# First stage of a two-layer model: projections in the order keys, queries, values; heads loaded for four rows at once; squares summed on TensorE

## The chip, the cores and the metric

The kernel runs on one core of one Trainium2 chip. The metric is the time on the device in microseconds (us) for one execution; the time before is the median of three runs.

## The reference

The reference is a model of two layers; the change lies in layer 0, in the part ahead of a recurrence.

```python
x = _layernorm(hidden_states)                       # 8 rows of 512 tokens, 128 channels
q = l2norm(silu(short_conv(x @ Wq.T, cq)).reshape(b, l, 16, 8))
k = l2norm(silu(short_conv(x @ Wk.T, ck)).reshape(b, l, 16, 8))
v = silu(short_conv(x @ Wv.T, cv)).reshape(b, l, 16, 8)
lr = softplus(x @ Wlr.T + 1e-3)
# 32 chunks of 16 tokens, each step needs the state of the one before:
#   two softmaxes over the state, an output, two rounds of an attention-like update
o = lax.scan(step, (W_in0, W_out0), chunks(q, k, v, lr))
attn = layernorm_per_head(o) * (x @ Wg.T) @ Wo.T
# mixture of experts on the same x: top 2 of 8 experts for each of 4096 tokens
logits = x @ W_router.T ; gates = top2(softmax(logits))
y = sum over experts of gate * (silu(x @ Wg_e) * (x @ Wu_e)) @ Wd_e
```

Layer 1 (a state-space scan and a second mixture of experts with a capacity) follows, and its code is not touched beyond two counts of a semaphore.

## The kernel before

The kernel is written engine by engine: SP issues the hardware DMAs, GpSimd (POOL) the scatters, and each engine's program is an order written out by hand, with semaphores between them. Nothing is planned by a program: what stands first in an engine's block runs first.

**Stage A, layer norm.** SP loads `x` in four pieces of 512 KB (L530 to L532), then seven small weights, then the three expert weights of 2 MB each (L538). VectorE waits for all four pieces (L1633), takes statistics of 32 tiles (L1545, L1548) and writes 32 normalised tiles (L1554). TensorE transposes them in groups of four (L860), ScalarE copies them to `xnT` (L1176). POOL meanwhile issues 28 DMAs of 260 KB that clear the slot tables (L711, L714).

**Stage B, projections and convolutions.** There are 24 units, numbered `cu`: for each of the eight rows b the query, the key and the value projection in turn (L865 to L870). A unit is a 128x512 product on TensorE into one of four banks, a first tap on ScalarE (L1188) into one of four buffers `cv`, three more taps on VectorE (L1642), SiLU on ScalarE (L1180), and a store of 256 KB to the DRAM scratch `qkv_scr` (L557). The first tap of unit cu waits until the store of unit cu-4 has landed, since both use one buffer (L1187). Once per row TensorE also makes the gate (L874) and the learning rates (L875), and SP loads the heads of the row before back from DRAM, in the layout of the recurrence, where partition (b, h) holds 8x512 values: K, V and Q of 256 KB each into the 16 partitions of that row (L545), and the learning rates (L548). SP's queue is one list: loads and stores are issued in this order.

**Stage C, routing.** After the last unit TensorE computes the router's logits for 32 tiles (L845, called at L877). VectorE then runs `dispatch(0)` (L1563 to L1620): softmax with one exponential on ScalarE (L1201), top 2, a mask, ranks by two matmuls (L851, L852, awaited at L1590), and the slots (`slots_ready`, L1620). POOL waits for the slots and issues 64 indirect DMAs (L727) that scatter the normalised rows to their slots. SP loads the first tiles of slots once all 64 have landed (L569, L574).

**Stage D, unit length.** ScalarE squares K (L1208) into `TMP`, VectorE sums over the 8 elements (L1654), and the same for Q with the one buffer; then root (L1211), reciprocal (L1658) and product (L1659). The learning rates pass through Abs, Exp and Ln on ScalarE (L1214 to L1216), and VectorE finishes them (L1661). SP waits for both sums before it loads expert tiles (L570), because `TMP` and the tiles share memory.

**Stage E, the recurrence.** 32 steps, mostly on VectorE (`step`, L1696 to L1823). Steps 4 to 27 are routed: TensorE, ScalarE and POOL run three expert tiles beside each step. The last step without tiles, step 3, already transposes the first tile: on TensorE `xg_T(4, 0)` and `up(4, 0)` stand ahead of `o_sums(3)` (L944 to L953), and on ScalarE the copy `xT(c + 1, 0)` stands ahead of the exponential `exp_q` (L1279 to L1281), for which VectorE waits at L1756. Two reciprocals stand in each half of a step: Z3 and ZK (L1725, L1727), Z2 and ZQ (L1796, L1759). In a routed step ScalarE writes the last result tile of the step before (`y(c - 1, 2)`, L1269) ahead of a table load and three SiLUs (L1271 to L1273), and then loads the table for the exponential `exp_2` (L1274, L1278), for which VectorE waits at L1792.

ScalarE enters step 0 after SP's 4 MB fill of `y_tok1` (L568) has landed (L1297), and TensorE enters it after the three expert weights (L881).

Of the kernel before, what the change touches and what calls it, by code (L numbers as in the profile page):

```python
# [107 lines left out]
def build(nc, d):  # L108
# [5 lines left out]
    with ExitStack() as ctx:  # L114
# [10 lines left out]
        qkv_scr = dram("qkv_scr", [3, P, T])  # L125
        lr_scr = dram("lr_scr", [2 * H, T])
# [76 lines left out]
        TMP = xnT[:].rearrange("p (e t) -> p e t", e=HD)  # L203
# [51 lines left out]
        MK, MQ, ZK, ZQ = (sb(n, [P, CH]) for n in ("MK", "MQ", "ZK", "ZQ"))  # L255
        M2, M3, Z2, Z3 = (sb(n, [P, 2 * DI]) for n in ("M2", "M3", "Z2", "Z3"))
# [51 lines left out]

        x_loaded = sem("x_loaded")
# [9 lines left out]
        xn_ready = sem("xn_ready")  # L319
        xnT_ps = sem("xnT_ps")  # L320
# [12 lines left out]
        heads_loaded = sem("heads_loaded")  # L333
# [107 lines left out]
        NCU = 3 * B  # L441
        ZEROED = 16 * (TILES_A // 4 + E * CAP // (4 * P))
# [86 lines left out]
        def _(sp):  # L529
            for g in range(4):  # L530
                sp.dma_start(x[:, 8 * g:8 * g + 8, :],
                             d["x"].rearrange("(i p) c -> p i c", p=P)[:, 8 * g:8 * g + 8, :]).then_inc(x_loaded, 16)  # L532
# [4 lines left out]
            for dst, src in ((wg_a, "wg_a"), (wu_a, "wu_a"), (wd_a, "wd_a")):  # L537
                sp.dma_start(dst[:], d[src]).then_inc(we_loaded, 16)  # L538

            def heads_load(b):  # L540

                for w, dst in ((1, K), (2, V), (0, Q)):
                    cu = 3 * b + w
                    sp.wait_ge(stored[cu % 4], 16 * (cu // 4 + 1))
                    sp.dma_start(dst[b * H:(b + 1) * H, :, :],  # L545
                                 qkv_scr[w].rearrange("(h e) (b t) -> b h e t", h=H, b=B)[b]).then_inc(heads_loaded, 16)
                sp.wait_ge(lr_stored[b % 2], 16 * (b // 2 + 1))
                sp.dma_start(LZ[b * H:(b + 1) * H, :, :],  # L548
                             lr_scr.rearrange("(h j) (b t) -> b h j t", h=H, b=B)[b]).then_inc(heads_loaded, 16)

            sp.wait_ge(xn_ready, NT)
            for cu in range(NCU):
                b, w = divmod(cu, 3)
                sp.wait_ge(silu_done, cu + 1)
                sp.dma_start(qkv_scr[w, :, b * L:(b + 1) * L], cv[:, cu % 4, :]).then_inc(stored[cu % 4], 16)  # L557
                if w == 0 and b >= 1:
                    sp.wait_ge(lr_copied, b)
                    sp.dma_start(lr_scr[:, (b - 1) * L:b * L], LR[0:2 * H, (b - 1) % 2, :]).then_inc(lr_stored[(b - 1) % 2], 16)  # L560
                if w == 2 and b >= 1:
                    heads_load(b - 1)
            sp.wait_ge(lr_copied, B)
            sp.dma_start(lr_scr[:, (B - 1) * L:B * L], LR[0:2 * H, (B - 1) % 2, :]).then_inc(lr_stored[(B - 1) % 2], 16)
            heads_load(B - 1)
# [4 lines left out]
            sp.wait_ge(norm2, 2)  # L570
# [117 lines left out]
        def _(pool):  # L688
# [29 lines left out]
            pool.wait_ge(xn_ready, NT)  # L718
# [52 lines left out]
            pool.wait_ge(xn_ready, 2 * NT)  # L771
# [68 lines left out]
        def _(pe):  # L840
# [13 lines left out]
            for g in range(G4):  # L854
                if g >= 2:
                    pe.wait_ge(xnT_copied, g - 1)
                for j in range(4):
                    i = 4 * g + j
                    pe.wait_ge(xn_ready, i + 1)
                    t = pe.transpose(ps[:, g % 2, j * P:(j + 1) * P], xn[:, i, :], ident[:])  # L860
                t.then_inc(xnT_ps, 1)
            pe.wait_ge(w_loaded, 16 * 7)
            for b in range(B):
                rhs = xnT[:, b * L:(b + 1) * L]
                pe.wait_ge(xnT_copied, b + 1)  # L865
# [12 lines left out]
            ranks(0)

# [106 lines left out]
            def turn(g):  # L986

                pe.wait_ge(xn_ready, NT + 4 * g + 4)
# [178 lines left out]
        def _(act):  # L1167
# [6 lines left out]
            for g in range(G4):  # L1174
# [8 lines left out]
            for cu in range(NCU):  # L1183
# [5 lines left out]
                if cu >= 1:  # L1189
                    silu(cu - 1)  # L1190
# [878 lines left out]
```

## Time and profile before

| | us |
|---|---|
| median of three runs | 1404.48 |
| lowest and highest | 1402.98, 1407.38 |
| the profiled execution, its own time | 1406.85 |
| its span in the trace | 1404.7 |
| VectorE busy in the span | 1254.6 (89%) |
| TensorE busy | 986.4 (70%) |
| ScalarE busy | 693.6 (49%) |
| GpSimd busy | 686.5 (49%) |

The share of busy time is a mean over stages. The 2.15 us between the span and the execution's own time lie around the span and are taken as unchanged. Times in the views count from the start of the span. A view of one engine in order of time gives for each row its start, its length, the operation, and in brackets how long the engine sat idle before it and what ended that.

### The profile page before, as it was taken

The page shows a single profiled execution, that of the slowest core. Times are in us where ns is not written, and L with a number is a line of the kernel's source. Part 1 is how long each engine was busy: PE and PEld are TensorE (multiplying, and loading weights), DVE is VectorE, ACT ScalarE, POOL GpSimd, SP SyncE. Part 2 cuts the span into 40 slices and gives each one's busy share as a digit, 9 for nine tenths or more (in the row PEclk, how much of TensorE's full clock was granted, in tenths as well). Part 3 has the DMA queues.
Part 4 walks back from the last instruction along what each step waited for, and adds up shares of the span by engine and source line. Part 5 has one row for each costly group of instructions (what it writes and reads, how often), then busy time and mean ns, then how long its engine had stood idle before and what let it go on. Part 6 is the DMA issues. An engine that isn't in the chain of part 4 may idle for free. (4 is left out here: it accounts for less than half of the span.)

```text
span 1404.7 us, 15886 instructions
## 1 busy us (share of the span) xinstructions
PE 986.4 (70%) x3590; PEld 577.2 (41%) x3591; DVE 1254.6 (89%) x2399; ACT 693.6 (49%) x1297; POOL 686.5 (49%) x623
## 2 busy tenths in 40 slices
PE   4671134778877777777762587668988898888874
PEld 2131032455555555555552562223434443444331
DVE  6767999999999999999989988999897888879899
ACT  2541312455455554455532327636576667666742
POOL 5001874222322223222211005788798789788895
PEclk9875556798899899999975668988999899999998
DMA  9998111000000000000052304446354435444346
GB/s 366 250 180 184 40 44 41 14 22 23 19 22 19 17 23 19 20 19 18 14 152 91 90 1 142 139 142 183 131 179 148 163 130 170 137 163 159 105 176 189
DMA packets 110082, 145.48 MB, mean 104 GB/s; under 512 B 26843, under 2 KB 82920, under 8 KB 105552
## 3 DMA queue, kind: packets, MB, share of 16 engines
q1 hardware_dynamic: 94448, 118.70, 29.3%
q0 software_dynamic: 9920, 21.12, 4.1%
q10 hardware_dynamic: 5664, 5.11, 1.2%
q8 instruction: 16, 0.26, 0.1%
q14 instruction: 34, 0.28, 0.1%
HBM read 108.06 MB, written 39.04 MB: 105 GB/s over the span
## 5 line engine op out<-in xcount | busy, mean ns | idle before, releaser
L1961 DVE TENSOR_TENSOR ps<-ps,cv 128x512 f32<-128x512 f32 x256 | 163.1, 682 | 24.8 <-ACT ps L1499 23.5
L1072 PE MATMUL ps<-Q,ident 128*128 128x512 f32 x256 | 140.5, 641 | 34.3 <-DVE Q L1979 21.2
L750 POOL DMA_INDIRECT y_tok<-xnT,meta x72 | 76.8, 1067 | 147.1 <-ACT xnT L1238 140.0
L727 POOL DMA_INDIRECT slots_x<-xn,sl_put x64 | 76.0, 1188 | 133.5 <-DVE sl_put L1620 114.3
L806 POOL TENSOR_TENSOR Q<-LR,xn 128x512 f32<-128x512 f32 x96 | 122.7, 1278 | 28.7 <-DVE LR L1970 13.1
L911 PE MATMUL ps<-wd_a,xn 128*128 x576 | 97.7, 321 | 36.7 <-ACT xn L1232 36.7
L921 PE MATMUL ps<-x,ident 128*128 128x64 f32 x512 | 74.0, 298 | 61.9 <-DVE x L518 52.2
L523 POOL TENSOR_TENSOR x<-x 128x512 f32<-128x512 f32 x27 | 31.8, 1176 | 174.5 <-DVE x L1763 174.5
L921 PEld LDWEIGHTS ps<-x,ident 128*128 128x128 f32 x512 | 73.3, 218 | 76.3 <-DVE x L518 56.8
L911 PEld LDWEIGHTS ps<-wd_a,xn 128*128 128x128 f32 x576 | 82.4, 220 | 50.5 <-issue 49.0
L894 PE MATMUL ps<-wg_a,xnT 128*128 x144 | 93.9, 739 | 12.3 <-issue 10.9
L1250 ACT ACTIVATE x<-x 128x128 f32<-128x128 f32 (+1 forms) x127 | 32.0, 277 | 133.4 <-DVE x L1822 60.9
L1970 DVE TENSOR_TENSOR_SCAN LR<-V,ps 128x512 f32<-128x512 f32 x64 | 77.6, 1212 | 14.3 <-ACT V L1458 12.4
L901 PE MATMUL ps<-ident,xn 128*128 128x128 f32 x288 | 47.6, 291 | 56.7 <-DVE xn L1708 56.7
L929 PE MATMUL ps<-x,ident 128*128 128x128 f32 x256 | 43.2, 323 | 62.6 <-DVE x L523 31.6
L1077 PE MATMUL ps<-Q,ident 128*128 128x512 f32 x144 | 80.2, 644 | 7.1 <-POOL Q L817 4.2
L1970 DVE TENSOR_TENSOR_SCAN LR<-wd_a,ps 128x512 f32<-128x512 f32 x64 | 77.5, 1211 | 5.0 <-POOL Q L806 2.8
L1072 PEld LDWEIGHTS ps<-Q,ident 128*128 128x128 f32 x256 | 47.9, 202 | 80.4 <-DVE Q L1979 29.5
L895 PE MATMUL ps<-wu_a,xnT 128*128 x144 | 80.3, 642 | 0.0
L1970 DVE TENSOR_TENSOR_SCAN Q<-wd_a,ps 128x512 f32<-128x512 f32 x64 | 76.6, 1197 | 0.9 <-POOL seg L817 0.5
L1970 DVE TENSOR_TENSOR_SCAN Q<-V,ps 128x512 f32<-128x512 f32 x64 | 76.5, 1196 | 0.0
L1224 ACT ACTIVATE xnT<-ps 128x128 f32<-128x128 f32 x72 | 19.5, 272 | 113.9 <-PE ps L887 113.9
(340 smaller groups left out, 2773.2 us busy)
## 6 DMA issues: line engine op xcount, KB each, us to landing
cv<-bc_scr SPq DMA_DIRECT2D x64, 512.0 KB, 3.9
xn<-bc_scr SPq DMA_DIRECT2D x24, 1024.0 KB, 4.7
O<-bc_scr SPq DMA_DIRECT2D x8, 1024.0 KB, 5.0
slots_x<-O POOLq DMA_DIRECT2D x28, 260.0 KB, 11.2
qkv_scr<-cv SPq DMA_DIRECT2D x24, 256.0 KB, 6.4
xnT<-slots_x SPq DMA_DIRECT2D x72, 64.0 KB, 1.8
x<-in_x SPq DMA_DIRECT2D x8, 512.0 KB, 5.8
y_tok<-O SPq DMA_DIRECT2D x1, 4096.0 KB, 17.6
```

What stands on the lines that cost most here:

```text
L727: pool.indirect_dma_start(out=slots_x, out_offset=bass.IndirectOffsetOnAxis(ap=sl_put[:, j, i:i + 1], axis=0), in_=xn_rows[:, i, :], in_of ...
L750: pool.indirect_dma_start(out=y_tok, out_offset=bass.IndirectOffsetOnAxis(ap=meta_bits[:, n, 0:1], axis=0), in_=yg[:, k, :], in_offset=Non ...
L806: pool.tensor_tensor(yc_g0[:, n % 4, :], st_g0[:, n % 2, :], cn, ALU.mult).then_inc(yc_ready, 1)
L894: pe.matmul(ps[:, 1 + 2 * k, :], xgT[:, k, :], wg_a[:, bass.ds(off, F)], start=True, stop=True).then_inc(gu_ps, 1)
L895: pe.matmul(ps[:, 2 + 2 * k, :], xgT[:, k, :], wu_a[:, bass.ds(off, F)], start=True, stop=True).then_inc(gu_ps, 1)
L901: t = pe.transpose(ps[:, 1 + 2 * k, f * P:(f + 1) * P], hid[:, k, f * P:(f + 1) * P], ident[:])
L911: m = pe.matmul(ps[:, 0, 0:D], hidT[:, k, f * P:(f + 1) * P], wd_a[:, bass.ds(off + f * D, D)], start=(f == 0), stop=(f == FC - 1))
L921: m = pe.matmul(ps[:, 7, 0:DI * CH], ident[:], PQ[:, e, :, :], start=(e == 0), stop=(e == HD - 1))
L1072: pe.matmul(ps[:, 4, :], ident[:], yc_g0[:, n % 4, :], start=(n == 0), stop=(n == NS - 1)).then_inc(y0_used, 1)
L1077: pe.matmul(ps[:, 5, :], ident[:], yo_g1[(units_before(c) + u) % 3], start=(u == 0), stop=(u == units(c) - 1)).then_inc(y1_used, 1)
L1961: tt(dBu(g), ps[:, 2 + g, :], b_rows[:, n % 4, :], ALU.mult).then_inc((inject0, b_used)[g], 1)
L1970: dve.tensor_tensor_scan(st(n, g), dA(k), dBu(g), 0.0, ALU.mult, ALU.add).then_inc(scanned, 1)
```

## The change

- The 24 units come in the order of eight key, eight query, eight value units (`CONVS`). A transposition stands between the first units, the learning rates go with the queries, four tiles of logits with each value unit. The gate products come after the routing's ranks, into the banks of the units.
- `qkv_scr` is laid out `[3, B, P, L]`, so that a store is one contiguous block, and the heads are loaded in six DMAs of 1 MB, each for four rows b, into 64 partitions. A load is issued after units 5, 9, 13, 17, 21 and at the end. The learning rates come back in one DMA.
- The expert weights are loaded after the heads, two of the three after a sum of squares. The slot tables are cleared after `x` has landed. VectorE starts statistics on each quarter of `x`.
- VectorE normalises 16 tiles and ScalarE the other 16.
- Squares go to `wd_a` and `wu_a`; the sum over 8 elements is eight matmuls with the identity. The reciprocal for K stands inside `dispatch`, after the mask.
- SP waits for `gate_copied` where it waited for the sums.
- In a step, Z3 and ZK share one reciprocal, and so do Z2 and ZQ. ScalarE loads the SiLU table and runs the first SiLU ahead of `y(c - 1, 2)`.

The core of the diff:

```diff
+        CONVS = [(w, b) for w in (1, 0, 2) for b in range(B)]
+            def heads_load(half, w):
+                for cu in range(4):
+                    sp.wait_ge(stored[cu], 16 * (2 * (1, 0, 2).index(w) + half + 1))
+                dst, done = ((Q, q_in), (K, k_in), (V, v_in))[w]
+                sp.dma_start(dst[half * 64:(half + 1) * 64, :, :],
+                             qkv_scr[w, 4 * half:4 * half + 4].rearrange("b (h e) t -> (b h) e t", h=H)).then_inc(done, 16)
+            for cu, (w, b) in enumerate(CONVS):
+                sp.wait_ge(silu_done, cu + 1)
+                sp.dma_start(qkv_scr[w, b], cv[:, cu % 4, :]).then_inc(stored[cu % 4], 16)
...
+                if cu % 4 == 1 and cu > 4:
+                    n = cu // 4 - 1
+                    heads_load(n % 2, CONVS[4 * n][0])
...
+            heads_load(1, 2)
+            sp.dma_start(wg_a[:], d["wg_a"]).then_inc(we_loaded, 16)
+            for n, (dst, src) in enumerate(((wd_a, "wd_a"), (wu_a, "wu_a"))):
+                sp.wait_ge(norm2, n + 1)
                 sp.dma_start(dst[:], d[src]).then_inc(we_loaded, 16)
...
-            sp.wait_ge(norm2, 2)
+            sp.wait_ge(gate_copied, B)
...
+            for g in range(4):
+                pool.wait_ge(x_in[g], 16)
...
+            def norms(n, sq, bank):
+                pe.wait_ge(squared, 4 * n + 4)
+                for e in range(HD):
+                    m = pe.matmul(ps[:, bank, :], ident[:], sq[:, e, :], start=(e == 0), stop=(e == HD - 1))
+                m.then_inc(norm2, 1)
+            turn0(0)
+            turn0(1)
             pe.wait_ge(w_loaded, 16 * 7)
             for b in range(B):
+                project(b)
+                if b + 2 < G4:
+                    turn0(b + 2)
+            for b in range(B):
+                project(B + b)
+                since(pe, lr_copied, b)
+                pe.matmul(ps[0:2 * H, 7, :], wlr[:], xnT[:, b * L:(b + 1) * L], start=True, stop=True).then_inc(lr_ps, 1)
+            for b in range(B):
+                project(2 * B + b)
+                m = logits(0, range(4 * b, 4 * b + 4), wrt[:])
+            m.then_inc(logits_ps, 1)
+            norms(0, sq_k, 6)
             ranks(0)
+            norms(1, sq_q, 7)
+            for b in range(B):
+                pe.wait_ge(conv_done, NCU)
+                since(pe, gate_copied, b - 3)
+                pe.matmul(ps[:, 2 + b % 4, :], wproj[:, 3 * P:4 * P], xnT[:, b * L:(b + 1) * L], start=True, stop=True).then_inc(gate_ps, 1)
...
+            for cu in range(2, NCU):
+                if cu + 1 < G4:
+                    xnT_copy(cu + 1)
+                silu(cu - 2)
+                tap(cu)
+                if B <= cu < 2 * B:
+                    lr_copy(cu - B)
+                k = cu - 2 * B - 2
+                if 0 <= k < 4:
+                    if k == 0:
+                        act.wait_ge(k_in, 32)
+                    square(K, sq_k, 2 * k)
...
+            norm_roots(0, 6)
+            act.wait_ge(q_in, 32)
+            for k in range(4):
+                square(Q, sq_q, 2 * k)
+            for b in range(B):
+                if b == 4:
+                    norm_roots(1, 7)
+                act.wait_ge(gate_ps, b + 1)
+                act.activation(gateT[:, b * L:(b + 1) * L], ps[:, 2 + b % 4, :], ACT.Copy).then_inc(gate_copied, 1)
...
+                if here:
+                    act.preload_act_table(ACT.Silu)
+                    silu_gate(c, 0)
                 if before:
                     y(c - 1, 2)
                 if here:
-                    act.preload_act_table(ACT.Silu)
-                    for k in range(TPS):
-                        silu_gate(c, k)
+                    silu_gate(c, 1)
+                    silu_gate(c, 2)
...
+                    if i % 8 == 0:
+                        dve.wait_ge(x_in[i // 8], 16)
...
                 tt(mask, oh[:, 0], oh[:, 1], ALU.add).then_inc(mask_ready, 1)
+                if layer == 0:
+                    unit_length_root(0)
...
-                o.wait(z_3)
-                r_3 = o.mark(dve.reciprocal(Z3[:, j:], Z3[:, j:]))
                 o.wait(z_k)
-                r_k = o.mark(dve.reciprocal(ZK[:], ZK[:]))
+                r_k = o.mark(dve.reciprocal(Z3K[:, j:], Z3K[:, j:]))
```

## Rows read from the trace of the kernel before

**Rows 1.** VectorE's waits, whole span: us in total, times, longest.

```profile
DVE cv L1642 <- ACT cv L1188: 19.0, 7, 3.4
DVE Z L1793 <- ACT x L1250: 5.8, 13, 0.5
```

**Rows 2.** VectorE in order of time, stages A to D.

```profile
10.58 6.28 DVE L1545 BATCH_NORM_STATS2 stats<-x 128x6 f32<-128x128 f32 x32 [10.58 <-DMA x<-in_x]
...
20.01 8.30 DVE L1554 TENSOR_SCALAR xn<-x,mv,rstd 128x128 f32<-128x128 f32 x32
...
30.39 9.08 DVE L1642 SCALAR_TENSOR_TENSOR cv<-ps,taps,cv 128x511 f32<-128x511 f32 x12 [2.00 <-ACT cv L1188]
...
97.53 4.54 DVE L1642 SCALAR_TENSOR_TENSOR cv<-ps,taps,cv 128x511 f32<-128x511 f32 x6 [2.42 <-ACT cv L1188]
110.09 0.42 DVE L1563 COPY O<-ps 128x256 f32<-128x256 f32 x1 [8.02 <-PE ps L845]
...
124.56 0.42 DVE L1591 COPY O<-ps 128x256 f32<-128x256 f32 x1 [2.16 <-PE ps L852]
...
132.29 0.20 DVE L1620 CAST sl_put<-slot 128x64 int32<-128x64 f32 x1
132.40 7.02 DVE L1654 TENSOR_REDUCE nrm<-xnT 128x512 f32<-128x4096 f32 x1
...
150.66 3.35 DVE L1658 RECIPROCAL nrm<-nrm 128x512 f32<-128x512 f32 x1
154.05 4.42 DVE L1659 TENSOR_TENSOR K<-K,nrm 128x4096 f32<-128x4096 f32 x1
...
167.42 0.18 DVE L1685 COPY WI<-X 128x32 f32<-128x32 f32 x1
```

**Rows 3.** ScalarE in order of time, stages B and C.

```profile
68.51 0.69 ACT L1188 ACTIVATE cv<-ps,taps 128x512 f32<-128x512 f32 x1 [4.31 <-DMA qkv_scr<-cv]
...
102.76 1.28 ACT L1201 ACT_TABLE_LOAD   x1
```

**Rows 4.** DMA: GB/s in 40 slices of 60 to 80 us, then of 0 to 20 us.

```profile
GB/s 102 119 98 111 119 94 115 119 90 119 107 189 254 369 402 381 324 205 98 111 119 94 115 115 98 111 115 102 115 184 193 229 340 361 369 315 234 119 127 119
...
GB/s 0 0 0 20 126 306 346 332 307 285 287 297 291 286 268 184 342 411 327 383 412 414 406 413 419 412 391 397 408 413 391 396 402 392 376 377 378 365 427 525
```

**Rows 5.** POOL in order of time: the first scatter and a long one.

```profile
133.31 1.02 POOL L727 DMA_INDIRECT slots_x<-xn,sl_put  x1 [114.30 <-DVE sl_put L1620]
...
155.01 4.31 POOL L727 DMA_INDIRECT slots_x<-xn,sl_put  x1 [0.31 <-issue]
```

**Rows 6.** All engines in order of time, step 3 of the recurrence.

```profile
232.33 0.33 SPq L574 DMA_DIRECT2D xnT<-slots_x  x1
...
234.52 0.47 PE L887 MATMUL ps<-ident,xnT 128*128 128x128 f32 x1 [6.09 <-DMA meta<-slots_x]
...
235.21 0.25 ACT L1250 ACTIVATE x<-x 128x64 f32<-128x64 f32 x1
...
235.60 0.21 DVE L1757 TENSOR_REDUCE ZQ<-x 128x16 f32<-128x64 f32 x1
```

**Rows 7.** The stores, line L557: from issue to landing.

```profile
DMA to landing us min/median/max: 2.0/6.4/8.6
```

**Rows 8.** TensorE in order of time: two projections (each is two passes).

```profile
38.69 1.98 PE L870 MATMUL ps<-xnT,wproj 128*128 128x512 f32 x4
```

**Rows 9.** Stretch 80:110: us; busy of PE, PEld, DVE, ACT, POOL; PEclk; DMA share; GB/s.

```profile
80.00:110.00 30.00, 25.40 (x80) 16.37 (x80) 16.13 (x22) 12.63 (x21) 0.00 (x0) 0.64 1.06 178
```

**Rows 10.** DMA issues: the fill of 4 MB, median us from issue to landing.

```profile
y_tok<-O SPq DMA_DIRECT2D x1, 4096.0 KB, 17.6
```

**Rows 11.** VectorE in order of time, the second half of a routed step.

```profile
410.26 0.19 DVE L1796 RECIPROCAL Z<-Z 128x8 f32<-128x8 f32 x1
410.38 0.21 DVE L1757 TENSOR_REDUCE ZQ<-x 128x16 f32<-128x64 f32 x1
410.62 0.25 DVE L1759 RECIPROCAL ZQ<-ZQ 128x16 f32<-128x16 f32 x1
```

More of the change, by code:

```diff
@@ L305, in s1_of @@
             return s1_later[:, c * L:(c + 1) * L] if c else wproj[:]
+        x_in = [sem(f"x_in{g}") for g in range(4)]
         x_loaded = sem("x_loaded")
@@ L553, in _ @@
[L553 to L562, printed above, removed]
@@ L1173, in _, with norm_rows, xnT_copy, tap @@
             act.activation(rstd[:], rstd[:], ACT.Sqrt).then_inc(ln_std, 1)
-            for g in range(G4):
+            act.wait_ge(ln_bias, 1)
+            def norm_rows(g):
+                for i in range(4 * g, 4 * g + 4):
+                    act.activation(xn[:, i, :], x[:, i, :], ACT.Identity, scale=rstd[:, i:i + 1], bias=nrm[:, 0, i:i + 1]).then_inc(xn_act, 1)
+            def xnT_copy(g):
                 act.wait_ge(xnT_ps, g + 1)
                 act.activation(xnT[:, g * 512:(g + 1) * 512], ps[:, g % 2, :], ACT.Copy).then_inc(xnT_copied, 1)
+            def tap(cu):
+                act.wait_ge(proj_ps, cu + 1)
+                if cu >= 4:
+                    act.wait_ge(stored[cu % 4], 16 * (cu // 4))
+                act.activation(cv[:, cu % 4, :], ps[:, 2 + cu % 4, :], ACT.Copy, scale=taps[:, CONVS[cu][0], 3:4]).then_inc(tap_first, 1)
             def silu(cu):
@@ L1649, in _, with unit_length @@
             dispatch(0)
-            dve.wait_ge(heads_loaded, 16 * 4 * B)
-            for n in range(2):
-                dve.wait_ge(squared, n + 1)
-                dve.tensor_reduce(nrm[:, n, :], TMP.rearrange("p e t -> p t e"), AX_X, ALU.add).then_inc(norm2, 1)
+            def unit_length(n, t):
+                o.mark(tt(t[:], t[:], bc(nrm[:, n, :], 1, HD), ALU.mult))
+            dve.wait_ge(lr_landed, 16)
             dve.tensor_scalar_add(LZ, LZ, 1e-3).then_inc(lr_in, 1)
-            for n, t in enumerate((K, Q)):
-                dve.wait_ge(norm_root, n + 1)
-                o.link(dve.reciprocal(nrm[:, n, :], nrm[:, n, :]))
-                o.mark(tt(t[:], t[:], bc(nrm[:, n, :], 1, HD), ALU.mult))
+            unit_length(0, K)
+            unit_length_root(1)
+            o.wait()
+            unit_length(1, Q)
+            dve.wait_ge(v_in, 32)
             dve.wait_ge(lr_log, 1)
@@ L1758, in q_sum @@
                     o.wait(z_q)
-                    return o.mark(dve.reciprocal(ZQ[:], ZQ[:]))
+                    z = ZQ if alone else Z2Q[:]
+                    return o.mark(dve.reciprocal(z, z))
                 def q_apply(r_q):
@@ L1772, in step @@
                     q_softmax()
-                    q_apply(q_sum())
+                    q_apply(q_sum(alone=True))
                     o_product()
@@ L1794, in step @@
                 g_2 = o.mark(tt(G2, bc(kc, 1, 2 * DI), bc(E2, 2, HD), ALU.mult))
-                o.wait(z_2)
-                r_2 = o.mark(dve.reciprocal(Z2[:], Z2[:]))
                 q_apply(q_sum())
```

148 lines of the change are left out of this document (74 added, 74 removed).

## Prediction

> **What bounds the kernel now.** I read the busy shares first: VectorE is busy 89% of the span, so what it waits for is the place to look, and the change lies ahead of the recurrence. The table of waits [rows 1] names a wait of 19.0 us for ScalarE's first taps; VectorE in order of time [rows 2] shows three more holes, 10.58 us until `x` has landed, 8.02 us for the logits, 2.16 us for the ranks. Each is followed to what ends last behind it.
>
> *Convolutions.* 12 taps in a row take 9.08 us, so a unit costs VectorE 2.27 us and 24 units 54.5 us; they take from 30.39 to 102.07 [rows 2], 71.7 us. The taps are late because a buffer's store has not landed [rows 3]. The DMA view says why: between 60 and 80 us all engines move data, but in plateaus of about 110 GB/s of some 7 us each, with peaks near 400 [rows 4]. A plateau is K, V and Q of one row, 3 x 256 KB into 16 partitions (0.79 MB / 110 GB/s = 7.1 us). The stores leave at the peak, behind the loads. So stage B is bound by loads of heads that nobody needs yet.
>
> *Routing.* `dispatch` runs from 110.09 to 132.49 [rows 2]. POOL's first scatter starts at 133.31 [rows 5], and the first tile is loaded at 232.33 [rows 6]: 99.8 us after the slots.
>
> *Which chain is last?* The recurrence starts at 167.42 [rows 2] and reaches `q_sum` of step 3 at 235.60, 68.2 us later. That instruction needs an exponential that ScalarE issues behind the copy of the first expert tile: tile load 232.33, transposition 234.52, exponential over at 235.46, `q_sum` at 235.60 [rows 6]. In time, this is 3.3 us after the scatters. VectorE has hardly an idle moment there, so both chains end within about 0.1 us of each other. This is the main finding: before the routed steps there are two chains, **slots + 99.8 + 3.3** and **start of the recurrence + 68.2**, and what is gained on one alone is worth nothing.
>
> **The change part by part.**
>
> *Start.* Statistics start per quarter of `x`. Now all wait until 10.58; at over 300 GB/s, as seen before POOL's fills join, 2.1 MB need some 6.5 us from 2.1 us on [rows 4], so the last quarter lands near 9.2 and its 8 tiles take 6.28 / 4 = 1.6. VectorE ends at 10.8 instead of 16.86. Aggregation, root and reciprocal took 3.15 us to 20.01; one tiny product (0.2) is added: 14.2. I put nothing for the seven small weights, awaited here now, since the fills start later too; if they are late, up to 7 us go (bound: no gain). ScalarE takes half the rows and the copies besides; the first tap then comes at about 20.4 and VectorE's taps begin at 21 instead of 30.39.
>
> *Stage B.* Loads become six of 1 MB into 64 partitions. No row shows that shape; the nearest are 110 GB/s into 16 partitions (9.5 us each) and about 400 into 128 (2.6 us) [rows 4]. I take half of 400, as half of the partitions: 5.2 us. Per four units the queue then holds four stores of 0.65 us and one load, 7.8 us, below VectorE's 9.1 us, so VectorE is the bound again. A store's allowance is three units less SiLU and tap, 6.8 - 1.4 = 5.4 us; alone it lands in 2.0 [rows 7], behind a load in about 5. I add 4 us for such edges and the first units: 21 + 54.5 + 4 = **79.5**. With 2.6 us per load it would be 76, with 9.5 us 98.5 (each block of four then lasts 4 x 0.65 + 9.5 = 12.1 us).
> Of the page "SBUF — State Buffer" in the Trainium skill, the section "Door 1: The DMA port swizzle" says that 16 partitions reach 4 of 16 ports and that 64 reach 8, no more than 32 do. Its 109 GB/s for 16 agrees with the 110 here; for 64 it gives 218 GB/s, by which a load would take 4.8 us and the sum be the same to half a microsecond. It speaks against the full gain that 64 partitions seem to promise.
> TensorE: a projection is 0.99 us at full clock [rows 8], with a transposition, learning rates or four logit tiles beside it about 1.9 us per unit, under 2.27.
>
> *Routing.* Logits now lie beside the value units, so `dispatch` starts at the end of stage B, 79.6 (8.02 us of waiting gone). Two things lengthen it. The exponential's table load (1.28) was hidden in the wait [rows 3]; now it follows the last SiLU: +0.65. K's reciprocal, 3.35 [rows 2], takes the place of the 2.16 us wait for ranks: +1.2. The K sum (16 passes of 0.5 us from [rows 8]) stands ahead of the ranks on TensorE, but its squares end with the last units, so it is done near 80, while the mask takes a dozen us more. 22.4 + 0.65 + 1.2 = 24.25: slots at **103.9**, against 132.49: 28.6 us earlier.
>
> *Unit length.* Two sums of 7.02 leave VectorE [rows 2]. Q's sum on TensorE follows the ranks (14.6 us into `dispatch`), 8 to 16 us by clock; then four gate products, then ScalarE's root: about 30 us into `dispatch`. Two products and one reciprocal, 12.2, and the tail of the learning rates put the recurrence's start near 120, 17 us after the slots instead of 35. Weights and the fill of 4 MB now follow the second sum, 17.6 us to land [rows 10]: some 45 us into `dispatch`, 124, where ScalarE needs it. All of this hides under the scatters: recurrence 120 + 68.2 = 188.5, scatters 103.9 + 103.1 = **207.0**. 18.5 us of a new wait at `q_sum` of step 3, behind `exp_q`, eat what the sums on TensorE give. The scatter chain's own length I leave: its long ones (4.31 us against 1.0) fall on VectorE's K and Q products [rows 2, 5], and these stay beside scatters. Gain up to here: 235.6 - 207.0 = **28.6**.
>
> *Steps.* Merging Z2 with ZQ removes a slot of 0.12 us, but a reciprocal costs 0.19 for 8 elements and 0.25 for 16 [rows 11], so 24 cost 0.06 more, and this happens twice: nothing (bounds: a gain of 0.12 per half step, 6 us in all, a loss of 2). The earlier SiLU shortens ScalarE's list before `exp_2` by over half a microsecond; 5.8 us of waits in 13 cases hang on it [rows 1]. I take **5**.
>
> Sum: 28.6 + 5 = 33.6. The profiled execution took 1406.85, 2.4 above the median: 1406.85 - 33.6 = 1373.2; from the median 1370.9. I say **1372**.
>
> **The rivals.**
>
> *Loads stay at 110 GB/s* (the limit is the packet or the scratch, not the partitions). For: that rate is the only one seen for heads. Against: weights into 128 partitions run at 400. Stage B ends at 98.5, 19 us later: 1391. Chance 0.08.
>
> *TensorE falls to the low clock.* Of its two levels, 2.4 and 1.2 GHz, the mean over 80 to 110 us is 0.64 of full [rows 9], though busy 25.4 of 30 us, most of it the narrow logits. At 1.2 GHz 1.9 us of work per unit become 3.8, above 2.27: the last 16 units take 60 us instead of 36 and the result is 1396. Against: wide products now follow each other with gaps of 0.4 us. All of it 0.04; a part of it is in the range.
>
> *The scatters are not last* (the overlap of chains is looser than read): the start moves by 47 us, all of it gained: 1354. Against: row order of `exp_q`. Chance 0.04.
>
> *Slower: scatters against traffic.* Weights and the 4 MB fill now move while POOL scatters, from 24 to 45 us into `dispatch`, about 16 scatters. If each took the 4.31 us of the long row rather than 1.0 [rows 5], 16 x 3.3 = 53 us would end at 1425; it turns slower from 33.6 / 16 = 2.1 us extra each. Against: the long rows stand beside products on VectorE, not beside transfers, and POOL only has to issue. Chance 0.03.
>
> *The change does nothing*: a new wait (small weights, fills) takes what stage B gives. Chance 0.02.
>
> **How the numbers follow.** My case has 0.79. Its own range: loads between 2.6 us and 6, start of taps +-3, steps 0 to 11: 1360 to 1383. Taking in half of the slow loads and the clock: 1359 to 1386. A measurement tells 0.3%, 4 us, from no change. Faster 0.95, same 0.02, slower 0.03.
>
> **What would show it.** Taps on VectorE nearly unbroken from 21 us; GB/s in a head load about 200; `dispatch` starting within 1 us of the last tap, near 80; first scatter near 105, first tile load near 204; VectorE idle for 18 us at L1757's counterpart in step 3, behind ScalarE; waits for `exp_2` almost gone. Wrong if stage B ends after 90, if tile loading comes over 102 us after the slots, or if that idle time is missing.

## The result: 1388.4 us, and the profile after

The changed kernel takes **1388.39 us** (median of 4 runs, 1387.96 to 1389.55) against 1404.36 (4 runs, 1402.98 to 1407.38): a ratio of 0.9894, interval 0.9878 to 0.9910, so 16 us are gained by the medians and 15 by the ratio. Forecast were 33, and 1388.4 lies above the range of 1359 to 1386. The profiled execution took 1388.35 us with a span of 1386.6. One run of the kernel before, timed beside e8, e10 and e11 (below), took 2121.04 us and is left out as a slow one.

VectorE in order of time, stages A to D of the changed kernel (columns as in [rows 2]):

```profile
8.33 3.40 DVE L1618 BATCH_NORM_STATS2 stats<-x 128x6 f32<-128x128 f32 x16 [0.17 <-DMA x<-in_x]
...
15.00 4.19 DVE L1631 TENSOR_SCALAR xn<-x,mv,rstd 128x128 f32<-128x128 f32 x16
22.14 2.32 DVE L1723 SCALAR_TENSOR_TENSOR cv<-ps,taps,cv 128x511 f32<-128x511 f32 x3 [2.95 <-ACT cv L1222]
...
34.57 13.44 DVE L1723 SCALAR_TENSOR_TENSOR cv<-ps,taps,cv 128x511 f32<-128x511 f32 x18 [2.28 <-ACT cv L1222]
...
61.97 2.32 DVE L1723 SCALAR_TENSOR_TENSOR cv<-ps,taps,cv 128x511 f32<-128x511 f32 x3 [4.53 <-ACT cv L1222]
...
73.64 4.54 DVE L1723 SCALAR_TENSOR_TENSOR cv<-ps,taps,cv 128x511 f32<-128x511 f32 x6 [2.45 <-ACT cv L1222]
...
91.06 4.54 DVE L1723 SCALAR_TENSOR_TENSOR cv<-ps,taps,cv 128x511 f32<-128x511 f32 x6 [3.36 <-ACT cv L1222]
95.52 0.41 DVE L1645 COPY O<-ps 128x256 f32<-128x256 f32 x1
...
98.03 0.42 DVE L1651 TENSOR_REDUCE lmx<-O 128x32 f32<-128x256 f32 x1 [1.18 <-ACT O L1268]
...
108.43 3.35 DVE L1636 RECIPROCAL nrm<-nrm 128x512 f32<-128x512 f32 x1
...
119.35 0.20 DVE L1704 CAST sl_put<-slot 128x64 int32<-128x64 f32 x1
...
120.06 4.42 DVE L1734 TENSOR_TENSOR K<-K,nrm 128x4096 f32<-128x4096 f32 x1
...
127.78 4.42 DVE L1734 TENSOR_TENSOR Q<-Q,nrm 128x4096 f32<-128x4096 f32 x1
...
134.22 0.18 DVE L1768 COPY WI<-X 128x32 f32<-128x32 f32 x1
```

The taps begin 8.3 us earlier than in [rows 2], 1.1 later than forecast, and `dispatch` begins right behind the last tap. In between the taps are broken eleven times. They end at 95.5 us, 6.6 earlier than before, where 79.5 was forecast.

The waits of VectorE and ScalarE up to 240 us in the changed kernel (engine, line, what for: us in total, times, longest):

```profile
DVE cv L1723 <- ACT cv L1222: 21.8, 12, 4.5
ACT LR L1232 <- DMA lr_scr<-LR: 14.1, 6, 5.2
ACT cv L1222 <- DMA qkv_scr<-cv: 10.9, 5, 4.1
```

[rows 1] had 19.0 us in 7 for the first line. The wait has not gone, it has a second cause: ScalarE stands at L1232, where it copies the learning rates into one of two buffers, until the store of two units ago has landed, and the first tap of the next unit is queued behind that copy.

The second chain, all engines in order of time, at the end of step 3:

```profile
220.10 0.33 SPq L580 DMA_DIRECT2D xnT<-slots_x  x1
...
222.26 0.48 PE L921 MATMUL ps<-ident,xnT 128*128 128x128 f32 x1 [21.83 <-DMA meta<-slots_x]
...
222.95 0.25 ACT L1319 ACTIVATE x<-x 128x64 f32<-128x64 f32 x1
...
223.23 0.26 DVE L1838 TENSOR_REDUCE Z2Q<-x 128x16 f32<-128x64 f32 x1 [15.61 <-ACT x L1319]
```

VectorE enters the recurrence 33.2 us earlier than in [rows 2] (134.22 against 167.42), reaches `q_sum` of step 3 and sits idle there for 15.6 us, behind the exponential that ScalarE holds back for the first expert tile. The tile is loaded 12.2 us earlier than in [rows 6]: that, not the 33, is the gain of the stage. The forecast also missed a wait in step 0: VectorE stands there for 5.1 us (L1799, behind an exponential of ScalarE, which waits for the fill of `y_tok`), where nothing was put; the idle time at `q_sum` hides it.

The points of the two chains in each kernel, in us from the start of its span (the start of the row named; routed steps are steps 4 to 27, from the start of one to the start of the other; the experiments are explained below):

| kernel | last tap, `dispatch` | slots | first tile load | recurrence | `q_sum` of step 3 | routed steps | step 28 | span |
|---|---|---|---|---|---|---|---|---|
| before | 102.1, 110.1 | 132.3 | 232.3 | 167.4 | 235.6 | 464.2 | 23.1 | 1404.7 |
| after | 95.5 | 119.4 | 220.1 | 134.2 | 223.2 | 459.7 | 20.9 | 1386.6 |
| forecast | 79.5 | 103.9 | 203.7 | 120 | 207.0 | 459.2 | | 1371.1 |
| e1 | 90.2 | 114.0 | 213.8 | 128.9 | 217.0 | 459.2 | 23.1 | 1381.5 |
| e6 | 100.9 | 124.7 | 224.4 | 138.8 | 227.7 | 459.2 | 20.9 | 1390.3 |
| e12 | 80.9 | 104.7 | 204.6 | 118.8 | 207.7 | 459.2 | 21.0 | 1367.1 |
| e4 | 95.1 | 119.0 | 210.4 | 133.3 | 213.6 | 459.5 | 23.2 | 1378.4 |
| e5 | 89.7 | 113.5 | 207.5 | 128.3 | 210.8 | 459.5 | 20.9 | 1373.7 |
| e9 | 80.6 | 104.4 | 198.5 | 119.1 | 202.1 | 460.3 | 20.9 | 1364.7 |
| e10 | 79.4 | 103.3 | 194.8 | 117.8 | 197.8 | 460.5 | 23.0 | 1363.2 |
| e2 | 96.5 | 120.3 | 221.9 | 145.0 | 225.0 | 456.8 | 23.0 | 1386.9 |
| e3 | 101.2, 106.6 | 128.8 | 226.2 | 174.1 | 242.3 | 466.0 | 23.0 | 1412.8 |
| e7 | 96.7 | 120.5 | 221.3 | 135.5 | 224.8 | 467.0 | 23.8 | 1398.2 |
| e8 | 96.0 | 119.8 | 218.7 | 133.9 | 221.8 | 463.1 | 20.9 | 1388.3 |
| e11 | 101.4, 109.5 | 131.7 | 231.7 | 166.8 | 234.9 | 457.2 | 20.9 | 1397.3 |

Between the profiled executions the loss and gain is: 12.4 us up to `q_sum` of step 3, 4.5 in the routed steps, 2.2 in step 28, -1.0 elsewhere: 1404.7 - 1386.6 = 18.1. The forecast's 28.6 + 5 differs mainly by the first term.

### The profile page after: what moved, and what is told of

The parts are those of the page before. It is cut to its first block and busy times, and to the rows that moved or that the text cites. A ratio compares the mean times of both kernels' runs of the same rounds, so it can differ in the third digit from the quotient of the medians.

```text
span 1386.6 us, 15822 instructions
## 1 busy us (share of the span) xinstructions
PE 986.0 (71%) x3622; PEld 576.3 (42%) x3623; DVE 1236.4 (89%) x2319; ACT 697.6 (50%) x1319; POOL 686.1 (49%) x623
## 5 line engine op out<-in xcount | busy, mean ns | idle before, releaser
L1106 PE MATMUL ps<-Q,ident 128*128 128x512 f32 x256 | 137.8, 630 | 35.5 <-DVE Q L2059 22.4
L815 POOL TENSOR_TENSOR Q<-LR,xn 128x512 f32<-128x512 f32 x96 | 122.6, 1277 | 28.8 <-PE ps L1106 14.4
L945 PE MATMUL ps<-wd_a,xn 128*128 x576 | 96.8, 319 | 36.7 <-ACT xn L1301 36.7
L945 PEld LDWEIGHTS ps<-wd_a,xn 128*128 128x128 f32 x576 | 81.9, 219 | 49.5 <-issue 48.0
L928 PE MATMUL ps<-wg_a,xnT 128*128 x144 | 91.1, 720 | 12.7 <-issue 11.6
L2050 DVE TENSOR_TENSOR_SCAN LR<-V,ps 128x512 f32<-128x512 f32 x64 | 77.6, 1213 | 15.6 <-ACT V L1529 14.3
L955 PEld LDWEIGHTS ps<-x,ident 128*128 128x128 f32 x512 | 73.4, 218 | 40.9 <-DVE x L524 21.9
L1111 PE MATMUL ps<-Q,ident 128*128 128x512 f32 x144 | 79.2, 637 | 7.1 <-POOL Q L826 4.2
L929 PE MATMUL ps<-wu_a,xnT 128*128 x144 | 79.5, 636 | 0.0
L963 PEld LDWEIGHTS ps<-x,ident 128*128 128x128 f32 x256 | 41.8, 236 | 86.5 <-DVE x L529 38.1
```

Source lines behind the costliest of these rows:

```text
L815: pool.tensor_tensor(yc_g0[:, n % 4, :], st_g0[:, n % 2, :], cn, ALU.mult).then_inc(yc_ready, 1)
L928: pe.matmul(ps[:, 1 + 2 * k, :], xgT[:, k, :], wg_a[:, bass.ds(off, F)], start=True, stop=True).then_inc(gu_ps, 1)
L929: pe.matmul(ps[:, 2 + 2 * k, :], xgT[:, k, :], wu_a[:, bass.ds(off, F)], start=True, stop=True).then_inc(gu_ps, 1)
L945: m = pe.matmul(ps[:, 0, 0:D], hidT[:, k, f * P:(f + 1) * P], wd_a[:, bass.ds(off + f * D, D)], start=(f == 0), stop=(f == FC - 1))
L955: m = pe.matmul(ps[:, 7, 0:DI * CH], ident[:], PQ[:, e, :, :], start=(e == 0), stop=(e == HD - 1))
L963: m = pe.matmul(ps[:, 7, 0:HD * CH], ident[:], OP[:, r, :, :], start=(r == 0), stop=(r == DI - 1))
```

## The experiments

Each kernel was timed beside the kernel before on the same chip, whose medians were 1401.7 to 1405.5 us, in the last run 1414.8. So ratios are compared, and points inside the traces.

**Which chain is last.** Three reciprocals of `nrm` that nobody needs stand ahead of the recurrence; their three rows take 10.13 us. Once in the changed kernel (e2), once in the kernel before (e3).

```diff
+            for _ in range(3):
+                o.link(dve.reciprocal(nrm[:, 0, :], nrm[:, 0, :]))
             dve.wait_ge(zeroed, ZEROED)
```

> The changed kernel with three useless reciprocals of 128x512 (3.35 us each, 10.1 us in all) on VectorE just ahead of the recurrence. Theory of two chains: the scatters are last by 15.6 us, so the time stays at 1388 and the idle time at q_sum of step 3 falls from 15.6 to about 5.5 us. Rival (the recurrence is last, the idle time is a by-product): 1398.

> The kernel before with the same 10.1 us. Theory: there both chains end together, so the delay shows in full: 1414 to 1415, and the first tile waits for VectorE rather than for the scatters. Rival (the scatters are last there too, by a margin that the trace hides): less than 1410.

Measured: e2 1389.02 us (1388.68 to 1394.73), ratio 0.9918 (0.9894 to 0.9942), 3 us more than the change's 0.9894 by the ratios, with intervals that overlap; e3 1412.54 (1410.78 to 1415.03), 1.0068 (1.0051 to 1.0085), so 9.5 us on top of before (7 to 12 by the interval). VectorE at `q_sum` of step 3, first in e2, then in e3:

```profile
225.00 0.26 DVE L1840 TENSOR_REDUCE Z2Q<-x 128x16 f32<-128x64 f32 x1 [11.74 <-ACT x L1319]
```

```profile
242.27 0.21 DVE L1759 TENSOR_REDUCE ZQ<-x 128x16 f32<-128x64 f32 x1
```

In e3 no idle time stands there: the recurrence is last. And since 9.5 of the 10.1 us show in the time, before had hardly any slack. In e2 11.7 us are still left, not the 5.5 that 15.6 - 10.1 gives, because the delay also swallowed the 5.05 us for which step 0 of the changed kernel waits for the fill of `y_tok`, and the tile came 1.8 us later. Both together show the two chains of the prediction: before they tie, after the change the scatters are last by some 15 us. What the sums on TensorE give VectorE, two of 7.02 us [rows 2], is less than the 15.6 and 5.1 us that it waits, so by this estimate it is worth nothing here; no run puts them back.

**The learning rates' buffers (e1).** The copies go to eight blocks of `gateT`, which is free until the gates are made, so that ScalarE doesn't wait for a store there; one wait for all eight stores stands ahead of the gates' copies.

```diff
                 act.wait_ge(lr_ps, b + 1)
-                if b >= 2:
-                    act.wait_ge(lr_stored[b % 2], 16 * (b // 2))
-                act.activation(LR[0:2 * H, b % 2, :], ps[0:2 * H, 7, :], ACT.Copy).then_inc(lr_copied, 1)
+                act.activation(gateT[0:2 * H, b * L:(b + 1) * L], ps[0:2 * H, 7, :], ACT.Copy).then_inc(lr_copied, 1)
...
+            for k in range(2):
+                act.wait_ge(lr_stored[k], 16 * B // 2)
             for b in range(B):
```

> The changed kernel, with the learning rates copied into eight blocks of gateT instead of two of LR, so that no copy waits for a store. Theory: units 8 to 17 are paced by the two buffers (VectorE idle 12.3 us there); stage B ends near 84 instead of 95.5, slots, scatters, tile load and end all come 12 us earlier: about 1376. Rival (the 1 MB head loads hold the queue and the stores of cv would be late anyway): stage B ends above 92, time above 1384.

Measured: 1383.09 us (1381.18 to 1384.49), 0.986 (0.9844 to 0.9877): 5 us better, and the last tap came 5.3 us earlier, not 12. ScalarE's wait in e1 (as above), then a load and the store behind it in SP's queue in order of time, then the load issued between 36 and 52 us (size, us from issue to landing):

```profile
ACT cv L1222 <- DMA qkv_scr<-cv: 16.1, 5, 4.1
```

```profile
40.64 0.54 SPq L549 DMA_DIRECT2D K<-qkv_scr  x1
42.37 0.32 SPq L556 DMA_DIRECT2D qkv_scr<-cv  x1
```

```profile
K<-qkv_scr SPq DMA_DIRECT2D x1, 1024.0 KB, 8.9
```

The store issued at 42.37 lands 7.6 us later, at 49.98, where ScalarE's first tap of unit 10 starts behind it.

With the one wait away, the other grew from 10.9 to 16.1 us: stores of `cv` that are queued behind a load of 1 MB. So the two causes overlapped, and the loads are the deeper one.

**The shape of the loads (e6).** e1 with each load of 1 MB as four of 256 KB into 16 partitions each.

```diff
-                sp.dma_start(dst[half * 64:(half + 1) * 64, :, :],
-                             qkv_scr[w, 4 * half:4 * half + 4].rearrange("b (h e) t -> (b h) e t", h=H)).then_inc(done, 16)
+                for b in range(4 * half, 4 * half + 4):
+                    sp.dma_start(dst[b * H:(b + 1) * H, :, :],
+                                 qkv_scr[w, b].rearrange("(h e) t -> h e t", h=H)).then_inc(done, 16)
...
```

> e1_lr8 with each load of 1 MB into 64 partitions undone into four of 256 KB into 16 partitions, at the same places. Theory: a load of 1 MB then takes 9.5 us at 110 GB/s instead of about 6, stage B ends some 15 us later (near 105), and the time is 1398. Rival (the rate doesn't depend on the partitions): 1383.

Measured: 1391.83 us (1390.11 to 1392.07), 0.9918 (0.9899 to 0.9936), last tap at 100.9, 10.7 later than in e1 (15 were expected). The prediction's own case of loads at 110 GB/s had 98.5. The DMA view of e6, 36 to 80 us in 40 slices:

```profile
GB/s 220 19 238 0 283 209 223 15 223 15 223 7 158 395 214 7 218 259 179 119 119 119 119 119 30 220 397 248 0 266 73 257 194 45 194 45 194 6 114 367
```

The same view of the changed kernel, 36 to 90 us:

```profile
GB/s 194 85 109 194 303 194 206 135 376 193 6 82 319 182 218 194 194 73 0 212 30 11 232 0 179 71 308 231 194 137 387 205 0 194 340 194 194 143 325 402
```

The stretch of 119 in e6 is the plateau of [rows 4] again; the level to which the changed kernel returns is 194. So the change did what it says, 64 partitions move 1.6 times what 16 do, and the rival of loads that stay at 110 GB/s falls. The size of one load does not explain it: with pieces of 256 KB into 64 partitions e12 (below) moves 250 GB/s on average from 40 to 80 us, e6 159 from 36 to 80. For 64 partitions I had put 200 GB/s; that stands.

**The loads cut in four (e12, e9).** What is left is how long a store stands behind a load. Each 1 MB load becomes four of 256 KB, all into 64 partitions (two of the eight elements each), and one follows each unit's store (those of the last load come together at the end). So the loads are both cut and spread; which of the two does it was not tried apart. e12 is e1 with this; e9 has the edit of e4 (below) too.

```diff
-                if cu % 4 == 1 and cu > 4:
-                    n = cu // 4 - 1
-                    heads_load(n % 2, CONVS[4 * n][0])
+                if cu > 4:
+                    n, q = divmod(cu - 5, 4)
+                    heads_load(n % 2, CONVS[4 * n][0], (q,))
...
```

> e5_both with each load of 1 MB cut into four of 256 KB, each still into 64 partitions (two of the eight elements), one after each unit. Theory: a store of cv waits in the queue behind the whole load issued before it (7.6 us to landing for the store of unit 6), so short loads take the four holes of about 3 us from stage B: it ends near 82 instead of 90, the time is 1368 to 1370. Rival (the queue is short of bandwidth, not of order): stage B ends near 90, 1376.

> The change as it was made, with both faults of its stage B mended (learning rates in eight blocks, loads cut in four) and nothing else: the reciprocals stay in SBUF. Theory: the two faults are all that the prediction missed, and the rest of its sum stands. Then the last tap ends near 80.5 us (79.5 forecast), the slots are ready near 104.5 (103.9), the scatters take what they take in the changed kernel, so the first tile is loaded 100.5 later, at 205, and q_sum of step 3 stands at 208 (207.0) with some 16 us or more of idle time ahead of it; the median is 1388.4 - (223.2 - 208) = 1373 us, where the prediction said 1372. Rival 1: part of the gain of the run with both cures comes from PSUM in another way than through the scatters, so that this kernel stays above 1378. Rival 2: with earlier loads the chain of scatters is no longer last, and the time is the 1365 of the kernel with all three edits.

Measured: e9 **1364.86 us** (1363.34 to 1366.42), 0.9726 (0.9708 to 0.9744), the best kernel of this study: by the ratios 38 us below before (37 against the median on its own chip) and 24 below the change. e12 1372.99 (1368.82 to 1384.71), 0.9719 (0.9668 to 0.9771), beside 1414.8 of the kernel before on that chip. VectorE in e12:

```profile
34.47 40.14 DVE L1726 SCALAR_TENSOR_TENSOR cv<-ps,taps,cv 128x511 f32<-128x511 f32 x54 [2.29 <-ACT cv L1225]
76.42 4.54 DVE L1726 SCALAR_TENSOR_TENSOR cv<-ps,taps,cv 128x511 f32<-128x511 f32 x6 [1.81 <-ACT cv L1225]
80.88 0.42 DVE L1648 COPY O<-ps 128x256 f32<-128x256 f32 x1
...
207.72 0.26 DVE L1841 TENSOR_REDUCE Z2Q<-x 128x16 f32<-128x64 f32 x1 [15.72 <-ACT x L1322]
```

54 taps stand in one unbroken row, and the last ends at 80.9, with the 79.5 of the forecast; slots at 104.7 (103.9), `q_sum` of step 3 at 207.7 (207.0) behind 15.7 us of idle time (18.5). With the two faults of stage B mended, the prediction's points come out to within 1.5 us each; the idle time is 2.8 us shorter than forecast, since step 0 waits 4.8 us for the fill here too. The median of 1373 agrees with the forecast only in number: by the ratio, e12 stands at 1365 on the scale of 1404.4. That is not the second rival's doing, since 15.7 us of idle time say that the scatters are still last; the routed steps are no shorter than in e1, and of the 14.4 us between the spans of e1 and e12, 9.2 lie ahead of `q_sum`, 2.1 in step 28 and 3 behind it, on another chip. So e9 and e12 are compared inside the traces alone: `q_sum` of step 3 comes 5.6 us earlier in e9. TensorE's clock is higher too. The stretch of the convolutions, first in the changed kernel, then in e12 (columns as in [rows 9]):

```profile
40.00:95.00 55.00, 44.78 (x121) 19.29 (x121) 38.14 (x53) 27.82 (x46) 0.00 (x0) 0.79 0.67 186
```

```profile
40.00:80.00 40.00, 37.73 (x127) 16.55 (x126) 36.98 (x52) 27.93 (x46) 0.00 (x0) 1.00 0.82 250
```

Granted clock 1.00, the 2.4 GHz level, instead of 0.79. In the changed kernel TensorE is busy for only 1.15 us between 55 and 60, during the longest wait, and its clock, 0.98 there, is 0.50 from 60 to 65 us, the 1.2 GHz level. So here it fell right behind a wait, and in part the low clock is, as far as these two traces show, a consequence of the waits. That is not all: from 80 to 95 us TensorE is busy 14.1 us of 15 at 0.50 to 0.60, and why is open. It cost nothing here: the waits of ScalarE that the trace lists between 30 and 96 us are for stores and for VectorE, none is for TensorE, so the rival of the low clock falls for stage B.

**The two long scatters (e4, e5).** The first scatters of the changed kernel, POOL in order of time:

```profile
120.37 5.00 POOL L736 DMA_INDIRECT slots_x<-xn,sl_put  x1 [94.53 <-issue]
125.68 1.00 POOL L736 DMA_INDIRECT slots_x<-xn,sl_put  x1 [0.31 <-issue]
...
128.26 4.79 POOL L736 DMA_INDIRECT slots_x<-xn,sl_put  x1 [0.30 <-issue]
```

Each long one begins just behind a product of 4.42 us on VectorE (120.06, 127.78) and ends just after it. e4 writes the two reciprocals to PSUM, so that the products have one operand there; e5 has the edits of e1 and e4.

```diff
-                o.mark(dve.reciprocal(nrm[:, n, :], nrm[:, n, :]))
+                o.mark(dve.reciprocal(ps[:, 6 + n, :], nrm[:, n, :]))
...
-                o.mark(tt(t[:], t[:], bc(nrm[:, n, :], 1, HD), ALU.mult))
+                o.mark(tt(t[:], t[:], bc(ps[:, 6 + n, :], 1, HD), ALU.mult))
```

> The changed kernel with the reciprocals of the K and Q norms written to PSUM, so that the two products of 4.4 us read one operand from SBUF and one from PSUM. Theory (two operands in SBUF hold POOL back): the two scatters of 5.0 and 4.8 us shrink to 1.0, the chain of scatters to about 93 us, the time to 1380 to 1381. Rival (any long operation of VectorE on SBUF holds POOL, or the products themselves get slower from PSUM): 1388 or more.

> The changed kernel with both edits, the eight blocks for the learning rates and the reciprocals in PSUM. Theory: both act on the scatter chain, so they add: 5.3 and 6.9 us less than 1388, 1376 to 1377; the idle time at q_sum of step 3 stays near 4 us, so the recurrence is still not last. Rival (the recurrence, held by the 4 MB fill, becomes last): 1380.

Measured: e4 1381.53 us (1380.21 to 1389.39), 0.9869 (0.9838 to 0.9901); e5 1374.17 (1373.1 to 1375.4), 0.9793 (0.9776 to 0.9811). POOL in e4:

```profile
119.99 1.01 POOL L736 DMA_INDIRECT slots_x<-xn,sl_put  x1 [94.14 <-issue]
121.31 1.00 POOL L736 DMA_INDIRECT slots_x<-xn,sl_put  x1 [0.30 <-issue]
122.61 0.97 POOL L736 DMA_INDIRECT slots_x<-xn,sl_put  x1 [0.31 <-issue]
123.88 0.97 POOL L736 DMA_INDIRECT slots_x<-xn,sl_put  x1 [0.30 <-issue]
```

No long scatter is left; slots to first tile load fell from 100.7 to 91.4 us. 7.8 of the 9.3 are the two rows (5.00 + 4.79 against 2 x 1.0), the rest other scatters that vary between 0.96 and 1.9. The products take 4.41 as before. By the page "SBUF — State Buffer" of the Trainium skill, section "Who interferes with whom", a VectorE instruction with two inputs in SBUF contends with a GpSimd instruction that reads SBUF; with at most one such input, outside its two-port modes, it does not. e4 agrees, 5.00 against 1.01 us. `q_sum` of step 3 comes 9.7 us earlier in e4 than in the changed kernel, and 6.2 earlier in e5 than in e1. By the medians it is 7 to 9 us (1388.4 to 1381.5, 1383.1 to 1374.2), by the ratios 3.5 and 9.4. VectorE's idle time there falls to 4.2 us in e4, since the recurrence now also waits 7.7 us in step 0 for the fill: beyond those 4 us the scatters would no longer be last.

**The order of SiLU and y (e7, e11).** e7 is the changed kernel with the old order of ScalarE in the routed steps, e11 the kernel before with the new one.

```diff
-                if here:
-                    act.preload_act_table(ACT.Silu)
-                    silu_gate(c, 0)
                 if before:
                     y(c - 1, 2)
                 if here:
-                    silu_gate(c, 1)
-                    silu_gate(c, 2)
+                    act.preload_act_table(ACT.Silu)
+                    for k in range(TPS):
+                        silu_gate(c, k)
```

> The changed kernel with the order of ScalarE's SiLU and y(c - 1, 2) of a step undone. Theory: the waits of 0.5 us for exp_2 come back in every second routed step and cost 4.5 us: 1393. Rival (the merged reciprocals brought the 4.5 us of the routed steps): 1388.

> The kernel before with the new order of SiLU and y(c - 1, 2) alone. Undoing it in the changed kernel cost 9 us, 7.3 in the 24 routed steps and 2.8 in the step after them. Theory: it brings as much here, 1393 to 1395, with the waits of 0.5 us for exp_2 gone and fewer steps of 19.8 us in which TensorE is at its lower clock. Rival (only the waits of 0.5 us go, the rest is chance of phase): 1396 to 1397.

Measured: e7 1397.42 us (1395.41 to 1399.95), 0.9965 (0.9949 to 0.9981); e11 1392.71 (1390.0 to 1399.53), 0.9918 (0.9894 to 0.9942). By the ratios the order alone is worth 11 us to before (8 to 15 by the interval) and, from 0.9894 to 0.9965, 10 us in the changed kernel, and not 5. VectorE's waits over the whole span, for `exp_2` (L1873 and L1875) and for the exponential in the other half of a step (L1797 and L1799), and one in step 28 (L1861), in e7, then in the changed kernel, where the last is missing:

```profile
DVE Z3K L1797 <- ACT x L1319: 11.3, 15, 5.1
DVE Z2Q L1873 <- ACT x L1319: 6.7, 16, 0.5
DVE x L1861 <- ACT wproj L1335: 2.9, 1, 2.9
```

```profile
DVE Z3K L1799 <- ACT x L1319: 12.3, 11, 5.1
DVE Z2Q L1875 <- ACT x L1319: 0.3, 1, 0.3
```

The 6.4 us of `exp_2` were meant, and they are most of the 7.3 by which the routed steps are longer in e7; between before and e11 it is 5.8 of 7.0. TensorE over the routed steps, in e7, then in the changed kernel:

```profile
232.00:699.00 467.00, 370.98 (x1777) 256.59 (x1777) 439.50 (x888) 236.51 (x525) 128.54 (x118) 0.87 0.07 19
```

```profile
230.00:690.00 460.00, 354.09 (x1786) 247.84 (x1785) 437.69 (x889) 234.64 (x525) 127.92 (x118) 0.92 0.08 19
```

A routed step takes 18.9 us, and 19.7 to 20.0 where TensorE falls to 1.2 GHz for part of it (the eight products of L945 then take 2.07 us instead of 1.15). Such steps are 10 of 24 in e7, with 7 more of about 19.4; in the changed kernel 6 and none. These are not a second gain on top of the waits: in the changed kernel a slow step loses its 0.8 to 1.0 us at L1799, in e7 it mostly loses 0.3 to 0.5 at L1797 and as much again for `exp_2`, and the wait at L1797 and L1799 is no shorter with the new order (11.3 and 12.3 us). Before, e3 and e7 have routed steps of 464.2, 466.0 and 467.0 us; all eleven kernels with the new order 456.8 to 463.1. Step 28 is 23.8 us in e7 and 20.9 in the changed kernel, where the wait of 2.9 us (L1861) is missing; but it is 21 us in only seven of the eleven and 23 in the others, as with the old order, so that this part comes from the order is not shown. The 11.6 us between the two spans are then 7.3 in the routed steps, 2.9 in step 28 and 1.6 ahead of `q_sum` of step 3, where the edit changes nothing, less 0.2 elsewhere. Of e11 the profiled execution is the slowest of its six (1399.53 against a median of 1392.71), so its points show less than its median does. Whether and how the order keeps the clock up was not tried.

**The merged reciprocals (e8, e10).** e8 is the changed kernel, e10 is e9, with each reciprocal by itself again.

```diff
+                o.wait(z_3)
+                r_3 = o.mark(dve.reciprocal(Z3[:, j:], Z3[:, j:]))
                 o.wait(z_k)
-                r_k = o.mark(dve.reciprocal(Z3K[:, j:], Z3K[:, j:]))
+                r_k = o.mark(dve.reciprocal(ZK, ZK))
...
```

> The changed kernel with the merged reciprocals undone. Theory (a reciprocal of 24 elements takes 0.30 us against 0.25 for 16, and the slot that is saved is 0.12 us in one half step only): no change that can be told, 1386 to 1390. Rival 1 (the merge brings something): 1392. Rival 2 (with the SiLU order undone the routed steps took 467.0 us against 464.2 before, so the merge costs 3 us): 1385.

> e9_quarters with the merged reciprocals undone. As for e8_unmerged: within 2 us of e9_quarters (1365) by the first theory, 3 us less by rival 2.

Measured: e8 1391.54 us (1389.79 to 1393.78), 0.9912 (0.9891 to 0.9932); e10 1367.26 (1364.97 to 1370.16), 0.9743 (0.972 to 0.9765). Beside the ratios with the merge, 0.9894 and 0.9726, each is 0.0018 higher, 2.5 us; the intervals overlap in both pairs. A gain of 2 to 3 us beside e8 is likely, and not shown. And e8 does not bring back the step of before: a routed step at its shortest takes 18.97 us in e8 and e10, 18.90 in the changed kernel, and 18.87 before, where nothing is merged. What the merge is worth to before is open; by these steps it is nothing.

## Why the prediction missed, step by step

- **Where it failed: the end of stage B.** "I add 4 us for such edges and the first units: 21 + 54.5 + 4 = **79.5**". The taps began at 22.1 and took 54.5; the sum of the waits between them is 21.8 - 2.95 = 18.9, not 4. That is 1.1 + 14.9 = 16.0 us too late, and the points of the chain follow: slots 15.5 late, `q_sum` of step 3 16.2 late, the result 16.4 late. The prediction's own sign of being wrong, an end of stage B after 90, is there.
- **First part of it, a wait that was not priced.** The change had been read as "the learning rates go with the queries", and their two buffers were left out: one copy per unit instead of one per three, each behind a store on SP's queue. Removing it gave 5.3 us (e1), less than its 14.1 us of waits, since the second part came up behind it (10.9 us to 16.1).
- **Second part, the allowance of a store.** "alone it lands in 2.0 [rows 7], behind a load in about 5". A load's rate was sized rightly (200 put, plateaus of 194 seen), but from issue to landing it takes 7.8 to 8.9 us, and a store behind it as long: one issued 2 us after a load, at 42.4 in e1, landed after 7.6 us, where the allowance is 5.4. The 5.2 us were size over rate, with nothing for the way from issue to landing. The comparison that the queue's mean load, 7.8 us per four units, stays under 9.1 was right (e12 moves the same bytes under unbroken taps) and did not help: what counts is the longest that a store stands behind one transfer. Cutting and spreading the loads gave 9.3 us more (e1 to e12, 90.2 to 80.9). Together that is 14.6 of the 16.0.
- **Right: two chains, the later one counts.** e2 and e3 show both. The forecast idle time of 18.5 us at `q_sum` was 15.6. That they are near is in part luck: the recurrence started 14 us late, the tile came 16 late, and step 0 waited 5.1 us for the fill of `y_tok`, which the forecast let land just in time.
- **Right: routing.** `dispatch` 24.0 us against 24.25, with 1.18 us behind the table load and K's reciprocal in the place of the ranks' wait; slots to tile load 100.7 against 100.0 before, from row start to row start (the forecast's 99.8 counts from the row's end). Weights and fill did not lengthen the scatters, so the slower rival falls; a few scatters took 1.4 to 1.9 us, as in the kernel before (1.4 to 2.0).
- **The steps were sized too small**: 5 us for the new order, 10 to 11 by the medians (e7, e11). The waits for `exp_2` that were counted are 6.4 and 5.8 us; the traces show 7.0 to 7.3 us in the routed steps and 2 to 3 in step 28, which the forecast left out. In the profiled executions of the change itself steps 4 to 28 give 6.7. Why the two parts, 12 us of the stage and 10 of the order, come to 16 rather than 22 in the medians stays open in part: the stage and the merge without the order (e7) are worth only 0.0035 of before, 5 us, because that run's routed steps took 467.0 us, 2.8 more than before's, with more steps at the low clock (10, against 5 of 19.8 us or more before).
- **The range** ended at 1386 with loads up to 6 us. It had a bound for the rate of the loads but none for a second wait in the same stage.
- **Slips in the working that changed nothing**: 6.5 us of loading from 2.1 us on end at 8.6, and the text goes on with 9.2; the recurrence at 120 is 16 us behind slots at 103.9, and the text has 17.

## What to carry over

When a change moves work into fewer, denser units, go through every buffer that is reused there, and count how many units lie between two uses, not only the buffer named in the table of waits. On one DMA queue, a small transfer that others wait for costs what the transfer ahead of it costs (7.6 us behind one of 8.9 here, against 2.0 alone): cut that one into pieces between the small ones. And before pricing a gain, find the chains that end together, since only the later one pays.

## What the runs showed of the chip that was not expected

- In these traces a product of 4.4 us on VectorE with both operands in SBUF holds a scatter of POOL for its whole length (5.00 us instead of 1.01); with one operand in PSUM neither engine is slower. The prediction saw that the long scatters fall on the products, and left them alone; the two rows are worth 8 us of the chain.
- The same 1 MB moves at about 194 GB/s into 64 partitions and 119 into 16. Those queued behind pay for the rate (the last tap 10.7 us later in e6) and for the length of one transfer (9.3 us earlier in e12).
- TensorE's granted clock differed with the waits of stage B, 0.79 against 1.00, and with the order of ScalarE's list in the routed steps, 0.87 against 0.92, though neither edit touches TensorE. What links them was not tried.
- One reciprocal of 24 elements takes 0.30 us, one of 16 0.25: merging in both halves of every step gave 2.5 us by the ratios beside e8 and e10, which the intervals do not tell from nothing.
